# Batch statistics taken from raw filter sums, one joint scale and shift per batch, and logits on all partitions with a mask

## The reference

```
xn  = group_norm(x, 32 groups of 16 channels)        # over channel, row and column
y1  = sum over rows h of xn * w1[c, h]                # [b, c, W]
y2  = sum over columns w of xn * w2[c, w]             # [b, c, H]
z1, z2 = relu(batch_norm(y1)), relu(batch_norm(y2))   # over b and the 256 values, per channel
dot[c, b] = sum_k z1[b, c, k] * z2[b, c, k]           # H = W = 256
num = softmax((dot.reshape(2, 512) @ lw1.T + lb1) @ lw2.T + lb2)
out = x + xn * num[:, :, None, None]
```

## Time and profile before

| | us |
|---|---|
| Median of 3 runs | 1706.61 (1706.28 to 1708.42) |
| Profiled execution | 1705.58 |
| Its span, first to last instruction | 1703.8 |
| Outside the span | 1.8 |

### The profile page before, as it was taken

The page is one execution under the profiler, slowest core; times in us unless marked ns, Lnnn a source line. Parts: engine busy times, 40 slices in busy tenths (PEclk is TensorE's granted clock), DMA queues, the critical chain, the costliest instruction groups (busy, mean ns, idle before and its releaser), DMA issues.

```text
span 1703.8 us, 14430 instructions
## 1 busy us (share of the span) xinstructions
PE 485.6 (28%) x3416; PEld 169.7 (10%) x3416; DVE 1004.7 (59%) x2672; ACT 665.1 (39%) x517; POOL 508.9 (30%) x489
## 2 busy tenths in 40 slices
PE   3588766660223321223333243430000000000000
PEld 1123212120001100001001021210000000000000
DVE  5899999967757576776666786772222222222220
ACT  4688887856435455544445546600000000000000
POOL 7678787820315444443254000000000000000000
PEclk8799878885666665666566566665555555555555
DMA  9999999989999999999999999999999999999999
GB/s 393 426 425 427 427 428 426 428 338 419 432 428 431 431 430 431 430 432 430 432 430 430 431 428 430 430 385 431 431 432 431 432 431 431 432 431 432 431 431 408
DMA packets 52126, 723.80 MB, mean 425 GB/s; under 512 B 6241, under 2 KB 6753, under 8 KB 8034
## 3 DMA queue, kind: packets, MB, share of 16 engines
q1 hardware_dynamic: 33922, 458.84, 63.4%
q10 hardware_dynamic: 18144, 264.25, 36.3%
HBM read 454.63 MB, written 268.44 MB: 424 GB/s over the span
## 4 chain that ended last, share of the span: by engine, by line
DMA 39%; another core or an unknown queue 26%; DVE 8%; PE 3%; issue 2%; ACT 2%; SPq 1%; DVEq 1%; POOL 0%; ACTq 0%; POOLq 0%
DMA xs<-in_x 28%; DMA out<-xs 11%; DVE xs L1104 3%; PE ps_part L576 2%; DVE xs L1028 1%; DVE mul_junk L1002 1%; DVE y2s L1031 1%; SPq L378 1%; ACT xs L878 1%; PE ps_part L710 1%; ACT sq_junk L805 1%; DVEq L1002 0%; DVE xs L1002 0%; POOL rstd_b L468 0%
## 5 line engine op out<-in xcount | busy, mean ns | idle before, releaser
L805 ACT ACTIVATE sq_junk<-xs 128x4096 fp8e5<-128x4096 f32 x128 | 463.1, 3618 | 203.9 <-DMA xs<-in_x 198.6
L576 PE MATMUL ps_part<-xs,filters 128*32 128x512 f32 x1856 | 290.8, 781 | 525.3 <-DMA xs<-in_x 516.2
L1104 DVE TENSOR_SCALAR xs<-xs,scale,shift 128x4096 f32<-128x4096 f32 x90 | 222.8, 2496 | 353.9 <-DMA xs<-in_x 353.3
L1002 DVE SCALAR_TENSOR_TENSOR xs<-xs,ps_w 128x256 f32 (+1 forms) x832 | 294.5, 416 | 28.6 <-DMA xs<-in_x 18.4
L534 POOL TENSOR_TENSOR xs<-xs,w_late 128x2048 f32<-128x2048 f32 x40 | 179.6, 4526 | 102.6 <-ACT w_late L819 102.6
L878 ACT ACTIVATE xs<-xs,shift,scale 128x4096 f32<-128x4096 f32 x33 | 125.3, 3798 | 157.3 <-DVE xs L1104 135.5
L576 PEld LDWEIGHTS ps_part<-xs,filters 128*32 128x32 f32 x1856 | 79.3, 138 | 718.3 <-issue 718.3
L1028 DVE TENSOR_TENSOR xs<-xs,ps_w 128x4096 f32<-128x4096 f32 x26 | 114.7, 4413 | 52.8 <-PE ps_part L576 46.6
L468 POOL TENSOR_TENSOR rstd_b<-var,minus_half 128x2 f32<-128x2 f32 (+1 forms) x23 | 15.2, 661 | 417.2 <-DVE var L1054 417.2
L1022 DVE TENSOR_REDUCE y2s<-xs 128x8 f32<-128x2048 f32 x40 | 91.4, 2286 | 77.1 <-POOL xs L534 77.1
L439 POOL TENSOR_TENSOR xs<-xs 128x768 f32<-128x768 f32 x64 | 116.7, 1827 | 58.0 <-DMA xs<-in_x 55.0
(11 more groups left out here) (116 smaller groups left out, 458.4 us busy)
## 6 DMA issues: line engine op xcount, KB each, us to landing
xs<-in_x SPq DMA_DIRECT2D x209, 2048.0 KB, 24.0
out<-xs ACTq DMA_DIRECT2D x121, 2048.0 KB, 27.6
filters<-in_x SPq DMA_DIRECT2D x5, 2048.0 KB, 18.0
out<-filters ACTq DMA_DIRECT2D x5, 2048.0 KB, 86.2
xs<-in_lw SPq DMA_DIRECT2D x2, 2048.0 KB, 16.3
out<-xs SPq DMA_DIRECT2D x2, 2048.0 KB, 12.1
filters<-in_w_rows SPq DMA_DIRECT2D x1, 512.0 KB, 3.8
filters<-in_w SPq DMA_DIRECT2D x1, 512.0 KB, 8.9
```

The lines of the kernel that those rows point to most:

```text
L576: last = nc.tensor.matmul(ps_part[g % 2][32 * a:32 * a + 32, :], taps[:, g % 2, hf * JH + j, :], xs[:, s[0]:s[1] + 1:s[1] - s[0], j * W:(j ...
L805: nc.scalar.activation(sq_junk[:], xs[:, s, :], ACT.Square, accum_out=sq_sum[:, u % 2, u // 2, b:b + 1], saturate=False).then_inc(squared, 1)
L1002: return nc.vector.scalar_tensor_tensor(out=out, in0=x_row, scalar=1.0, in1=ps_w2[g % 2][:, 0:W], op0=ALU.mult, op1=ALU.mult, accum_out=total)
L1104: return nc.vector.tensor_scalar(buffer(s), buffer(s), scale[:, b, g:g + 1], shift[:, b, g:g + 1], ALU.mult, ALU.add)
```

## The change

It touches the statistics chain and the softmax; tiles, slots, loads and stores stay.

- **Batch statistics from raw sums.** `normalise` on ACT is gone. DVE takes `bn_stats` of ps_y1 and ps_y2 as they are, per batch (four of 256 values), aggregates four pairs, and works out the statistics of both batches together in eleven small instructions. The offset of a batch's group norm, `own_off`, is made by DVE in `group_moments`; its factor `own_rstd` by POOL, ahead of its other powers. POOL's `channel_factors` is one power.
- **One joint scale and shift.** A new DVE function, `channel_affine`, makes one scale and shift per batch and channel, then scales ps_y2 on DVE (two of 128 x 256). ACT's `rectify` goes from ps_y1 to `z` in two instructions of 128 x 256; the relu of ps_y2 is part of the dot product.
- **Logits on all partitions.** The dots are broadcast to 128 weight columns, so each partition holds all 512 logits. DVE masks them by `own` and sums over 16 channels (`logit_g`, 128 x 32), ACT takes the exponential of all 512 for the sum and of `logit_g`. The turning and spreading matmuls and their mask are gone; `coefficients` multiplies with the reciprocal in the same instruction.
- **Places.** `channel_moments` moves from stage 24 to 22 and `channel_affine` takes 25 in the first half (24, ahead of the tile, in the second); `rectify` from 27 to 26 (24); `dot_products` stays at 28 (27 in the second). POOL's `channel_factors` moves from 24 to 22, and in the second half ahead of the group's products. PE's fold of a quad's first group moves from the first to the second tile of its unit pair. `finish_row` makes the moments before the last fold, no longer waits for `bn_ready`, and has four matmuls without use ahead of the logits and none behind.

```diff
+                    nc.gpsimd.tensor_tensor(own_rstd[:], var[:, width - B:width], minus_half[:, 0:B], ALU.pow
+                                            ).then_inc(own_ready, 1)
...
-                then_wait(nc.gpsimd.tensor_tensor(bn_var[:], bn_mv[:, :, 1], eps[:], ALU.add))
-                then_wait(nc.gpsimd.tensor_tensor(bn_rstd[:], bn_var[:], minus_half[:, 0:2], ALU.pow))
-                if q:
-                    pool.wait_ge(relu_done, 2 * q)
-                then_wait(nc.gpsimd.tensor_tensor(bn_a[:], bn_rstd[:], affine[:, :, 0, q], ALU.mult))
...
-                nc.gpsimd.tensor_tensor(bn_b[:], affine[:, :, 1, q], bn_m[:], ALU.subtract).then_inc(affine_ready, 1)
+                pool.wait_ge(spread_ready, q + 1)
+                nc.gpsimd.tensor_tensor(bn_rstd[:], var_s[:], minus_half[:, 0:2], ALU.pow).then_inc(bn_ready, 1)
...
+                if g % QG == 2 and g // QG - 1 >= FQ:
+                    channel_factors(g // QG - 1)
...
+                    pe.wait_ge(z_done, 2 * q)
...
-                pe.wait_ge(dots_ready, 2 * (q + 1))
-                for b in range(B):
-                    last = nc.tensor.matmul(ps_l[0:1, :], dots[:, q, b:b + 1], mixed[:, B * h + b, :],
+                        pe.wait_ge(logits_taken, row)
+                    nc.tensor.matmul(ps_l[:], one[:].to_broadcast([1, P]), bias[:], start=True, stop=False)
+                for b in range(B):
+                    pe.wait_ge(dots_ready, 2 * q + b + 1)
+                    last = nc.tensor.matmul(ps_l[:], dots[:, q, b:b + 1].to_broadcast([P, P]), mixed[:, B * h + b, :],
                                             start=False, stop=(q % FQ == FQ - 1 and b == B - 1))
...
             def finish_row(row):
                 q = FQ * (row + 1) - 1
+                moments(batch_of(QG * (q + 1) - 1, 1))
                 fold_parts(QG * (q + 1) - 1)
-                moments(batch_of(QG * (q + 1) - 1, 1))
                 turn_rows(q)
-                pe.wait_ge(bn_ready, q + 1)
-                keep_warm(3)
+                keep_warm(4)
                 add_logits(q)
-                keep_warm(2)
-                spread_prob(row)
...
-                if hf == 0 and g % QG == 2:
-                    fold_parts(g - 2)
                 if hf and g:
+                    if g % QG == 2:
+                        fold_parts(g - 2)
...
-                for i, y in enumerate((z, ps_y2)):
-                    nc.scalar.activation(y[:], y[:], ACT.Relu, scale=bn_a[:, i:i + 1],
-                                         bias=bn_b[:, i:i + 1]).then_inc(relu_done, 1)
+                for b in range(B):
+                    half = slice(b * W, (b + 1) * W)
+                    nc.scalar.activation(z[:, half], ps_y1[:, half], ACT.Relu, scale=z_scale[:, 0, b:b + 1],
+                                         bias=z_shift[:, 0, b:b + 1]).then_inc(z_done, 1)
...
-                nc.scalar.activation(prob, ps_l[0:1, :], ACT.Exp, bias=neg_max[:], accum_out=exp_sum[:]
-                                     ).then_inc(exp_done, 1)
+                nc.scalar.activation(z[:], ps_l[:], ACT.Exp, bias=neg_max[:], accum_out=exp_sum[:]).then_inc(exp_done, 1)
+                act.wait_ge(logits_taken, row + 1)
+                nc.scalar.activation(logit_g[:], logit_g[:], ACT.Exp, bias=neg_max[:]).then_inc(powers_done, 1)
...
-                        if 2 * u + b == stage(q, 23):
-                            normalise(q)
...
+                q = quad_of(k)
+                if q is not None:
+                    nc.vector.tensor_tensor(own_off[:], nmean[:, width - B:width].unsqueeze(1).to_broadcast([P, 2, B]),
+                                            bc(tap_sum[:, q % 2, :, q // 2], B), ALU.mult)
...
+                dve.wait_ge(folded, QG * (q + 1))
+                dve.wait_ge(y2_turned, q + 1)
+                for i, y in enumerate((ps_y1, ps_y2)):
+                    for b in range(B):
+                        last = nc.vector.bn_stats(bn_st[:, B * i + b], y[:, b * W:(b + 1) * W])
+                then_wait(last)
+                for i in range(2 * B):
+                    last = nc.vector.bn_aggr(bn_mv[:, i], bn_st[:, i])
+                then_wait(last)
+                dve.wait_ge(own_ready, q + 1)
+                mean, spread_of = (bn_mv[:, :, i].rearrange("p (i b) -> p i b", b=B) for i in range(2))
+                rstd = own_rstd[:].unsqueeze(1).to_broadcast([P, 2, B])
+                nc.vector.tensor_tensor(mean_b[:], mean, own_off[:], ALU.add)
+                nc.vector.tensor_tensor(var_b[:], spread_of, rstd, ALU.mult)
+                then_wait(nc.vector.tensor_tensor(off_b[:], own_off[:], rstd, ALU.mult))
+                nc.vector.tensor_tensor(mean_b[:], mean_b[:], rstd, ALU.mult)
+                then_wait(nc.vector.tensor_tensor(var_b[:], var_b[:], rstd, ALU.mult))
+                nc.vector.tensor_tensor(mean_d[:], mean_b[:, :, 0], mean_b[:, :, 1], ALU.subtract)
+                nc.vector.tensor_tensor(mean_s[:], mean_b[:, :, 0], mean_b[:, :, 1], ALU.add)
+                then_wait(nc.vector.tensor_tensor(var_s[:], var_b[:, :, 0], var_b[:, :, 1], ALU.add))
+                then_wait(nc.vector.scalar_tensor_tensor(out=mean_d[:], in0=mean_d[:], scalar=0.5, in1=mean_d[:],
+                                                         op0=ALU.mult, op1=ALU.mult))
+                nc.vector.scalar_tensor_tensor(out=gap_b[:], in0=bc(mean_s[:], B), scalar=-0.5, in1=off_b[:],
+                                               op0=ALU.mult, op1=ALU.add)
+                nc.vector.scalar_tensor_tensor(out=var_s[:], in0=mean_d[:], scalar=2 * EPS, in1=var_s[:],
+                                               op0=ALU.add, op1=ALU.add).then_inc(spread_ready, 1)
+
...
+                rstd = own_rstd[:].unsqueeze(1).to_broadcast([P, 2, B])
+                dve.wait_ge(bn_ready, q + 1)
+                then_wait(nc.vector.scalar_tensor_tensor(out=bn_a[:], in0=bn_rstd[:], scalar=2.0 ** 0.5,
+                                                         in1=affine[:, :, 0, q], op0=ALU.mult, op1=ALU.mult))
+                nc.vector.tensor_tensor(z_scale[:], bc(bn_a[:], B), rstd, ALU.mult)
                 for i in range(2):
-                    dve.wait_ge(z_done, 4 * q + 2 * (i + 1))
-                    last = nc.vector.bn_stats(bn_st[:, i], (z, ps_y2)[i][:])
-                then_wait(last)
-                for i in range(2):
-                    last = nc.vector.bn_aggr(bn_mv[:, i], bn_st[:, i])
-                last.then_inc(bn_ready, 1)
+                    last = nc.vector.tensor_scalar(z_shift[:, i], gap_b[:, i], bn_a[:, i:i + 1], affine[:, i, 1, q:q + 1],
+                                                   ALU.mult, ALU.add)
+                last.then_inc(affine_ready, 1)
+                dve.wait_ge(affine_ready, q + 1)
+                for b in range(B):
+                    half = slice(b * W, (b + 1) * W)
+                    nc.vector.tensor_scalar(ps_y2[:, half], ps_y2[:, half], z_scale[:, 1, b:b + 1],
+                                            z_shift[:, 1, b:b + 1], ALU.mult, ALU.add).then_inc(y2_scaled, 1)
...
+                    half = slice(b * W, (b + 1) * W)
+                    dve.wait_ge(y2_scaled, 2 * q + b + 1)
+                    dve.wait_ge(z_done, 2 * q + b + 1)
                     nc.vector.scalar_tensor_tensor(
-                        out=z[:, b * W:(b + 1) * W], in0=z[:, b * W:(b + 1) * W], scalar=1.0,
-                        in1=ps_y2[:, b * W:(b + 1) * W], op0=ALU.mult, op1=ALU.mult,
-                        accum_out=dots[:, q, b:b + 1]).then_inc(dots_ready, 1)
+                        out=z[:, half], in0=ps_y2[:, half], scalar=0.0, in1=z[:, half],
+                        op0=ALU.max, op1=ALU.mult, accum_out=dots[:, q, b:b + 1]).then_inc(dots_ready, 1)
 
...
+                by_group = y_part[:, 0].rearrange("p (g c) -> p g c", c=CG)
                 dve.wait_ge(logits_ready, row + 1)
-                nc.vector.reduce_max(neg_max[:], ps_l[0:1, :], AX.X, negate=True).then_inc(exp_asked, 1)
+                nc.vector.tensor_tensor(by_group, ps_l[:].rearrange("p (g c) -> p g c", c=CG),
+                                        own[:].unsqueeze(1).to_broadcast([P, G, CG]), ALU.mult)
+                nc.vector.reduce_max(neg_max[:], ps_l[:], AX.X, negate=True).then_inc(exp_asked, 1)
+                dve.wait_ge(exp_asked, row + 1)
+                nc.vector.tensor_reduce(logit_g[:], by_group, AX.X, ALU.add).then_inc(logits_taken, 1)
                 dve.wait_ge(exp_done, row + 1)
-                nc.vector.reciprocal(exp_sum[:], exp_sum[:]).then_inc(prob_ready, 1)
...
+                then_wait(nc.vector.reciprocal(exp_sum[:], exp_sum[:]))
+                dve.wait_ge(powers_done, row + 1)
...
+                for t, fact in zip(of, facts):
+                    last = nc.vector.scalar_tensor_tensor(out=t, in0=fact, scalar=exp_sum[:], in1=powers,
+                                                          op0=ALU.mult, op1=ALU.mult)
...
```

(9 more changed lines are left out.)

140 lines of the change are left out of this document (41 added, 99 removed).

## The result

The changed kernel takes 1714.12 us in the median of 6 runs (1713.67 to 1715.85), the kernel before 1706.5 beside it: a ratio of 1.0041, interval 1.0031 to 1.0051. It is slower by some 7 us, outside the range (1701.6 to 1708.0). Its profiled execution took 1713.73, with a span of 1712.0. The change is 0.4%, and its interval is clear of 1.

The account below looks back on a forecast made before the run. Taken as bound by DMA traffic plus DMA idle time: a first-end chain 3.7 us shorter, less 1.0 for DVE's lateness, second end 0, gives 2.7 gained, 1706.61 to 1703.9 us; range 1701.6 to 1708.0.

Parts of the forecast that it names:

- From 360 to 372 us their share is 0.29: some 8.5 us idle: First softmax end: DMA engines idle some 8.5 us with all slots full, until the first scaled tile, started at 367.67.
- is as long as its traffic plus the idle time of the DMA engines: Whole kernel: traffic plus DMA idle time sets its length; work on other engines counts only where it leaves them idle.
- The third rival: Whole kernel: nothing moves the end, the first end's gain is handed back in the second half; 0, 1706.6 us; chance 0.15.
- DVE some 4 us late: End of the first half: DVE's added work for quads 0 to 2 makes it some 4 us late, bounds 2 to 7.
- DVE becomes the bound: First half: small steps at full duration, 6.4 late, 1707.1 us, chance 0.11; some steps doubled, 11 late, 1710.3, chance 0.07.
- Being late doesn't starve the DMA engines.: First half: over three tiles are queued behind each landing one, so DVE's lateness counts only where the turning waits for it.
- The chain, 11.1: First end, turned sums to first scaling: 11.1 us after the change against 14.8, so 3.7 us shorter.
- The rule weighed: Small DVE steps: waited ones 0.20 apart, unwaited 0.09, against the skill's rule that each waits for an emptied pipe.
- 3 of the 4 us are covered: Turning at the first end: PE's moments and last fold cover 3 us of DVE's lateness; turned sums come 1.0 later.
- Second end, 0: Second softmax end: chain some 2.5 us shorter, but loads cover it to 1130.3, so 0 gained, bounds 0 and 1.
- Last rows after 355: Wrong sign, end of the first half: DVE's last rows ending after 355, where near 352 was expected.
- A DMA share under 1 between 130 and 340 us: Wrong sign, first half: a DMA share under 1 there would mean that lateness starves the loads.

Follow-up runs that it names:

- leave: Changed kernel without DVE's statistics, small steps, affine and products for quads 0 to 2, constants instead: 1707.76 us, ratio 1.0000 to the kernel before.
- hybrid: Kernel before with the new statistics in quads 3 and 7 only, and the new logits and softmax: 1707.08 us, ratio 0.9997 to the kernel before.
- psum: Changed kernel with one input of each small DVE instruction in spare PSUM columns, five more of them per quad: 1711.32 us, ratio 1.0028 to the kernel before.
- late16: leave with 16 statistics without use per quad on DVE in place of the moments step of quads 0 to 2: 1707.97 us, ratio 1.0000 to the kernel before.
- after_short: Changed kernel without products, logits and softmax of quad 3, constants instead: 1709.89 us, ratio 1.0011 to the kernel before.
- actfree: Changed kernel with ACT's rectify of quads 0 to 2 on constants, not waiting for DVE's shift: 1716.15 us, ratio 1.0046 to the kernel before.
- psum_short: psum without products, logits and softmax of quad 3, constants instead: 1708.28 us, ratio 1.0001 to the kernel before.
- warm13: Kernel before with 13 matmuls without use in place of 3 ahead of the logits of quad 3: 1714.81 us, ratio 1.0041 to the kernel before.
- psum_warm9: psum with 9 matmuls without use in place of 4 ahead of the logits of quad 3: 1707.65 us, ratio 1.0003 to the kernel before.
- softmax_only: Kernel before with only the new logits and softmax: 1708.23 us, ratio 1.0001 to the kernel before.
- softmax_shift: softmax_only with 110 small matmuls without use on PE ahead of its work: 1707.87 us, ratio 1.0002 to the kernel before.

## Why the prediction was wrong, by its steps

- **"From 360 to 372 us their share is 0.29: some 8.5 us idle"**, and with it the kernel "is as long as its traffic plus the idle time of the DMA engines". This step failed for gains. The 8.5 us are a mean over 16 engines; one of them has none of it. A shorter stall was worth 0, not 2.7: leave and hybrid start the scaling 1.9 and 0.8 sooner and take the same time. The third rival, a gain handed back in the second half, names what these two do; how it is handed back is argued, not shown. For losses it does hold, from the point where the last engine runs dry.
- **"DVE some 4 us late", bounds 2 to 7.** Measured 12.4. 4.4 of it is the work as costed (psum, which has even five small instructions more); 8 is small instructions held by POOL: 0.91, 0.96 and 2.26 for 0.16. The step took 0.20 and 0.09 from rows beside which POOL stood still and used them where POOL works most of the time. The rival "DVE becomes the bound", in its form of 11 us late and 3.7 slower, was the nearest. It had the consequence right (later end of the rows, cover gone), but not the cause: it had steps on PSUM or the interrupted loop cost double, and steps with an input in PSUM are those that aren't held. That its lateness came so near the 12.4 is luck.
- **"Being late doesn't starve the DMA engines."** It did, from 341 on: 0.93, 0.52 and 0.47 to 362, while a slot for the next load comes free at 360.86 only. "More than three are queued" doesn't hold at 4 us late either: psum has 0.39 from 351 to 353. It was a hole without a cost of its own in late16, 6.1 us late.
- **The chain, 11.1.** Measured 12.7. Statistics 1.42 (1.4), aggregates 0.38 (0.4), eleven small ones 1.4 (1.5), power 0.70, logits 1.98 at full clock, softmax 3.1 (3.0): as forecast. The matmuls without use ran at half clock until 367, but nothing waited for them. The affine took 1.95 for 0.5, since L1038 and L1040 ran beside POOL's L402 and L404. The same cause again: POOL's own work, freed earlier by the change, stands beside the affine.
- **The rule weighed.** Small steps that nobody waits for start 0.07 to 0.08 apart in psum (142.67, 142.75, 142.82) and take 0.16: the overlap of the aggregates was read rightly, and nothing hung on it. The section cited there from the Trainium skill, page "VectorE: DVE Perf Modes", itself adds that a next instruction that isn't held starts earlier, so these rows don't contradict it.
- **"3 of the 4 us are covered", 1.0 on the turning.** With 12.4 late the turning began 9.4 later (361.15 for 351.80), so the cover of 3 was right. The sums came 10.2 later because the turning itself took 0.8 longer, at half clock; the step had taken its 1.1 from a row at full clock.
- **Second end, 0.** Right for this kernel: 387 GB/s for 384, first store at 1134.02 for 1128.04, shifted with the rest.
- **The signs named.** Last rows after 355 had been called a wrong sign, and came. A DMA share under 1 between 130 and 340 us did not: it is 1.01 from 100 to 340, and 1.00 at its lowest, where the traffic fell from 427 to 420 GB/s all the same. Window of after:

```profile
220.00:300.00 80.00, 50.57 (x370) 15.57 (x370) 79.02 (x446) 63.02 (x52) 64.68 (x73) 0.81 1.00 420
```

So of after's 7 us, 5 are the stretch 374 to 379 in which no engine has work, and after_short puts a price of 5.1 on it, give or take 2.4. The rest, 1.9 (0.2 to 3.6) by after_short, answers in size to the 1.7 lost before 340, which only after, after_short and actfree have. By the packet records that loss is for the most part not idle time (0.3 us) but slower packets: from 220 to 300 us 625 ns on the mean for 617, which is 1.0 us. That is an agreement of sizes, not a test, and the cause of the slower packets is open.

## What to carry to other kernels

Before idle time of the DMA engines is priced as a gain, look at the floor of its share: 0.06 and 27 GB/s mean that one engine of sixteen is still behind. A shorter stall then gave little or nothing in four kernels here, and 4.6 us in a fifth (psum_short), so run both the shorter and the longer stall. Price a small DVE instruction with two SBUF inputs by a row that has POOL running beside it, and put one input into PSUM where that row is long. Check a gain at one barrier at the next one, in GB/s per window, before believing it. Price matmuls at the clock that they will have: the turning took 1.94 us at half clock, for some 1.2.

## What the runs showed of the hardware that I had not expected

- An instruction on 128 x 2 or 128 x 4 elements took 0.15 to 0.17 us alone or with an input in PSUM, and up to 2.26 with both inputs in SBUF beside a running POOL instruction, ending where a POOL instruction ends (L1038, 2.26: past several of them, to 329.02).
- By the end of 340 us of full traffic one engine lags so far that it works 7 to 8 us alone (before: 363.7 to 371.0; warm13: 364.1 to 372.0), a packet of 16 KB each 0.61 us. Its cause is open; 2,100 more waits on SP cost no time (+0.5, interval -1.2 to 2.2).
- A stall made 2.4 us longer made a kernel 4.3 us faster (psum to psum_warm9), and one made 5.2 shorter made it 4.6 faster (psum to psum_short).
- Packets of 16 KB had a mean of 614.1 ns in before and 615.6 in psum_short, with the same bytes; that alone is 4.0 us for each engine.
- PE stopped for 0.9 to 3.5 us ahead of the last 17 of 64 equal matmuls in five kernels, and went on 1.3 to 1.4 us after a 16 KB packet of an instruction queue had ended. With 110 matmuls more ahead of it in the program the stop was gone from there (softmax_only to softmax_shift).
